# Weight-part rounding spread over eight sequences with its subtraction on GpSimd, biases and first values earlier, and the last-but-one rows through another PSUM bank, in a one-core attention and mixture-of-experts block

## The reference

```python
q = einsum('bse,hed->bhsd', x, Wq) + bq      # k and v likewise, 16 heads of 64
scores = where(causal, q @ k.T / sqrt(64), -inf)
out = softmax(scores) @ v ; out = out.reshape(32, 256, 1024) @ Wo + bo
x = layernorm(x + out)
xn = layernorm_affine(x, gamma, beta)
probs = softmax(xn @ router_w.T / 1.5)       # 8 experts, top 2
y = sum over the two experts of w_e * (silu(xn @ W1[e]) @ W2[e])
x = layernorm(x + y)
```

## Time and profile before

| | us |
|---|---|
| median of 3 runs | 1322.31 (1321.48 to 1324.12) |
| the profiled execution | 1320.37 |
| its span, first to last instruction | 1318.2 |
| PE busy | 1288.0 (98%) |
| DVE busy | 1102.1 (84%) |
| ACT busy | 1078.2 (82%) |
| POOL busy | 498.7 (38%) |

### The profile page before, as it was taken

How to read it: one execution, slowest core, us unless ns; L and a number is a source line. 1 busy time by engine, 2 the same in 40 slices (tenths; PEclk the granted TensorE clock), 3 DMA queues, 4 the chain that set the end, 5 groups by cost and what they waited for, 6 DMA issues and landing times.

```text
span 1318.2 us, 36163 instructions
## 1 busy us (share of the span) xinstructions
PE 1288.0 (98%) x11298; PEld 1141.5 (87%) x11298; DVE 1102.1 (84%) x5209; ACT 1078.2 (82%) x3481; POOL 498.7 (38%) x1067
## 2 busy tenths in 40 slices
PE   7999999999999999999999999999998999999997
PEld 6888888888888888888888888888887999999983
DVE  6888888888888888888888888888886898888856
ACT  7888888888888888888888888888885777777737
POOL 1013333333333333333333333333333675665645
PEclk9999999999999999999999999999998999999999
DMA  5011000000000000000000000000033587777748
GB/s 211 35 67 46 14 14 17 15 18 16 16 14 14 14 14 13 14 14 14 14 14 14 14 18 16 19 16 14 14 140 92 158 239 233 236 226 233 222 137 329
DMA packets 58860, 98.19 MB, mean 74 GB/s; under 512 B 9376, under 2 KB 36131, under 8 KB 58416
## 3 DMA queue, kind: packets, MB, share of 16 engines
q1 hardware_dynamic: 49024, 78.67, 19.2%
q0 software_dynamic: 8640, 17.13, 3.8%
q10 hardware_dynamic: 1008, 0.08, 0.1%
HBM read 65.85 MB, written 30.91 MB: 73 GB/s over the span
## 4 chain that ended last, share of the span: by engine, by line
PE 86%; ACT 6%; DVE 4%; issue 1%; DMA 1%; POOL 0%; ACTq 0%; SPq 0%; POOLq 0%; DVEq 0%
PE ps_f L1102 15%; PE ps_b L1136 13%; PE ps_a L1102 13%; PE ps_s L1143 12%; PE ps_s L1124 9%; PE ps_s L1102 7%; PE ps_a L1327 4%; PE ps_b L1327 4%; PE ps_s L1127 4%; ACT probs L596 2%; PE ps_s L1398 2%; ACT probs L598 2%; PE ps_a L1299 1%; PE ps_s L1148 1%; PE ps_f L1168 1%
## 5 line engine op out<-in xcount | busy, mean ns | idle before, releaser
L596 ACT ACTIVATE probs<-probs,neg_max 128x256 f32<-128x256 f32 x512 | 255.3, 499 | 134.7 <-DVE neg_max L845 134.7
L472 POOL TENSOR_SCALAR ln_b<-mv 128x2 f32<-128x2 f32 x32 | 6.1, 190 | 633.7 <-DVE mv L908 633.7
L841 DVE CUSTOM_DVE_ANT_0 probs<-ps_s,mask 128x256 f32<-128x256 f32 x512 | 214.2, 418 | 29.4 <-PE ps_s L1127 26.9
L1143 PE MATMUL ps_s<-ident,probs 128*128 128x128 f32 x1536 | 200.6, 274 | 0.9 <-issue 0.8
L1136 PE MATMUL ps_b<-pt,f_y 128*64 128x256 f32 (+1 forms) x2048 | 196.9, 334 | 3.5 <-ACT f_y L591 1.6
L598 ACT ACTIVATE probs<-probs,neg_max 128x128 f32<-128x128 f32 x512 | 198.7, 388 | 0.0
L855 DVE TENSOR_SCALAR probs<-probs,inv_sums 128x256 f32<-128x256 f32 x512 | 181.9, 355 | 9.1
L1136 PEld LDWEIGHTS ps_b<-pt,f_y 128*64 128x64 f32 x2048 | 132.6, 137 | 54.4 <-issue 9.6
L562 POOL DMA_INDIRECT y_tok<-f_y,m_dest x142 | 145.8, 1027 | 83.7 <-DVE m_dest L1008 57.2
L1124 PE MATMUL ps_s<-qk 64*128 64x256 f32 x1024 | 170.7, 409 | 5.3 <-ACT pt L631 3.0
L1143 PEld LDWEIGHTS ps_s<-ident,probs 128*128 128x128 f32 x1536 | 173.0, 143 | 1.6 <-issue 1.5
(11 more groups left out here) (205 smaller groups left out, 3144.4 us busy)
## 6 DMA issues: line engine op xcount, KB each, us to landing
m_w<-w_split SPq DMA_DIRECT2D x71, 512.0 KB
m_x<-queue SPq DMA_DIRECT2D x71, 133.0 KB
f_y<-y_tok SPq DMA_DIRECT2D x32, 256.0 KB, 6.6
queue<-empty SPq DMA_DIRECT2D x8, 532.0 KB, 4.8
x_raw<-in_x SPq DMA_DIRECT2D x32, 128.0 KB, 2.1
w_split<-f_y SPq DMA_DIRECT2D x8, 512.0 KB, 3.2
out_x<-f_y SPq DMA_DIRECT2D x16, 256.0 KB, 6.4
y_tok<-f_y,m_dest POOLq DMA_INDIRECT x142
```

Of the source, the lines that this page charges most:

```text
L596: act.activation(row[:, 0:2 * P], row[:, 0:2 * P], ACT.Exp, scale=-1.0, bias=neg_max[:, pair, h, 0:1], accum_out=sums[:, d % 2, pair, h, 0:1])
L841: dve.tensor_tensor_reduce(out=row[:, 0:2 * P], in0=ps_s[:, pair, h, 0:2 * P], in1=mask[:].rearrange("p a b -> p (a b)"), scale=-1.0, scal ...
L1143: ins = pe.transpose(ps_s[:, pair, h, dst:dst + P], probs[:, buf, pair, h, src:src + P], ident[:])
```

## The change

Five pieces.

1. Weight parts: ScalarE rounds one expert per sequence, at the end of step q = 1 of sequences 1 to 8, where eight consecutive steps held one each. The subtraction moves from VectorE to GpSimd's `step`, ahead of `norm`. SP stores the parts at q = 3 of these sequences.
2. Biases: `bq` and `bk` get semaphores of their own. VectorE scales bq first of all; ScalarE's first copy of q and k waits for bk and the scaled bq, and the other five small transfers are waited for later.
3. First values: at d = 0 VectorE copies the first half of the values out of `ps_f` ahead of `normalise(0, 0)`, where it stood behind.
4. The rows of sequence 30 (the last but one, at d = 127) are transposed behind both pairs' probabilities, into `ps_f`, where they stood ahead of them, in `ps_s`. `transpose_x(0)` moves up behind them, ahead of `step_outputs(LAST)`. ScalarE's `xnt` goes behind `first_pt(127)`.
5. On ScalarE `copy_outputs(127)` moves ahead of the second pair's exponentials, and `affine(0)` ahead of `copy_outputs(LAST)` and `first_pt(LAST)`; on VectorE `rest_of_x(0)` moves ahead of `second_pt(LAST)`.

```diff
 # SP
-                if n in (1, 2):
-                    e = d - QUADS
+                if q == 3 and 1 <= n <= E:
+                    e = n - 1
                     sp.wait_ge(w1_lo_done, e + 1)
 # GpSimd
+            def rest_of_w1(e):
+                pool.wait_ge(w1_hi_done, e + 1)
+                if e >= 2:
+                    pool.wait_ge(w1_stored[e % 2], e // 2 * 16)
+                pool.tensor_tensor(w1_part[:, e % 2, 1].bitcast(F32R), w1_raw[:, e], w1_part[:, e % 2, 0], ALU.subtract
+                                  ).then_inc(w1_lo_done, 1)
...
+                if q == 1 and 1 <= n <= E:
+                    rest_of_w1(n - 1)
-            pool.wait_ge(small_loaded, 16 * 7)
+            pool.wait_ge(small_loaded, 16 * 5)
 # ScalarE
+            act.dma_start(bq_raw[:], bq).then_inc(bq_loaded, 16)
+            act.dma_start(bk_sb[:], bk).then_inc(bk_loaded, 16)
...
-            act.wait_ge(small_loaded, 16 * 7)
+            act.wait_ge(bk_loaded, 16)
             act.wait_ge(biases_ready, 1)
             evacuate_qk(0, 0)
             evacuate_qk(0, 1)
+            act.wait_ge(small_loaded, 16 * 5)
...
+                if d == LAST - 1:
+                    copy_outputs(d)
                 if d < LAST:
                     for h in range(2):
                         exponentials(d, 1, h)
-                if q == 3 and n in MID:
+                if d == LAST - 1:
+                    first_pt(d)
+                    act.wait_ge(zt_ready, n)
+                    act.activation(xnt[:], ps_f[:, 0:S], ACT.Identity, scale=gamma_sb[:, 0:1],
+                                   bias=beta_sb[:, 0:1]).then_inc(xnt_done, 1)
+                if q == 3 and 1 <= n < SEQS - 1:
...
-                if n in (1, 2):
-                    e = d - QUADS
+                if q == 1 and 1 <= n <= E:
+                    e = n - 1
                     act.wait_ge(w1_loaded, 16)
...
+            affine(0)
             copy_outputs(LAST)
             first_pt(LAST)
-            affine(0)
             copy_outputs(LAST + 1)
 # VectorE
+            dve.wait_ge(bq_loaded, 16)
+            dve.tensor_scalar(bq_sb[:], bq_raw[:], SCALE, None, ALU.mult).then_inc(biases_ready, 1)
             rest_of_xt(1, 0)
             rest_of_weights(0, 0)
             rest_of_weights(0, 1)
-            dve.wait_ge(small_loaded, 16 * 7)
-            dve.tensor_scalar(bq_sb[:], bq_raw[:], SCALE, None, ALU.mult).then_inc(biases_ready, 1)
             rest_of_weights(0, 2)
+            dve.wait_ge(small_loaded, 16 * 5)
...
+                    if d == 0:
+                        evacuate_first_v(1, 0)
                     normalise(d, 0)
...
-                if n in (1, 2):
-                    rest_of_w1(d - QUADS)
...
+            rest_of_x(0)
             second_pt(LAST)
-            rest_of_x(0)
 # TensorE
-                if q == 3 and n in MID:
+                if q == 3 and 1 <= n < SEQS - 1:
                     pe.wait_ge(z_done, n)
...
+                if d == LAST - 1:
+                    pe.wait_ge(z_done, n)
+                    pe.wait_ge(res_done, n * TILES)
+                    for i in range(TILES):
+                        ins = pe.transpose(ps_f[:, i * P:(i + 1) * P], z[:, (n - 1) % 2, i, 0:D], ident[:])
+                    ins.then_inc(zt_ready, 1)
+                    transpose_x(0)
                 second_filler(n, q)
...
             step_outputs(LAST)
-            transpose_x(0)
             pe.wait_ge(max_done, LAST * 4)
```

More of the change, by code:

```diff
@@ L199, in postln_block @@
         attn_w_loaded = [sem("attn_w_loaded_%d" % i) for i in range(6)]
+        bq_loaded = sem("bq_loaded")
+        bk_loaded = sem("bk_loaded")
         small_loaded = sem("small_loaded")
@@ L577, in _ @@
         def _(act):
-            for dst, src in ((bq_raw, bq), (bk_sb, bk), (bv_sb, bv), (bo_sb, bo), (gamma_sb, gamma),
-                             (beta_sb, beta), (rw_sb, router_wt)):
+            act.dma_start(bq_raw[:], bq).then_inc(bq_loaded, 16)
+            act.dma_start(bk_sb[:], bk).then_inc(bk_loaded, 16)
+            for dst, src in ((bv_sb, bv), (bo_sb, bo), (gamma_sb, gamma), (beta_sb, beta), (rw_sb, router_wt)):
                 act.dma_start(dst[:], src).then_inc(small_loaded, 16)
@@ L656, in step @@
                     evacuate_qk(d + 1, 0)
-                if 1 <= d <= LAST:
+                if 1 <= d < LAST - 1:
                     first_pt(d)
@@ L660, in step @@
                     evacuate_qk(d + 1, 1)
-                if d >= 2 and q == 3:
+                if 2 <= d < LAST - 1 and q == 3:
                     copy_outputs(d)
-                if n in (1, 2):
-                    e = d - QUADS
+                if q == 1 and 1 <= n <= E:
+                    e = n - 1
                     act.wait_ge(w1_loaded, 16)
@@ L738, in rest_of_weights @@
                 ins.then_inc(attn_w_lo, 1)
[L740 to L745, removed]
             def rest_of_xt(count, par):
@@ L970, in step @@
                     rest_of_xt(n + 2, (n + 1) % 2)
-                if q == 0 and n < SEQS:
+                if q == 0 and 1 <= n < SEQS:
                     evacuate_first_v(n * 4 + 1, 0)
@@ L1169, in transpose_input, with transpose_x @@
                 ins.then_inc(xt_ready, 1)
+            def transpose_x(j):
+                pe.wait_ge(m_x_loaded[j % WBUFS], (j // WBUFS + 1) * 16)
+                if j >= 1:
+                    pe.wait_ge(m_xnt_done, j)
+                for i in range(BLOCKS):
+                    ins = pe.transpose(ps_a[:, 0, i * P:(i + 1) * P], m_x[:, j % WBUFS, i, 0:D], ident[:])
+                ins.then_inc(m_xt_ready, 1)
             def first_filler(n, q):
@@ L1292, in _ @@
             sequences(step)
-            def transpose_x(j):
-                pe.wait_ge(m_x_loaded[j % WBUFS], (j // WBUFS + 1) * 16)
-                if j >= 1:
-                    pe.wait_ge(m_xnt_done, j)
-                for i in range(BLOCKS):
-                    ins = pe.transpose(ps_a[:, 0, i * P:(i + 1) * P], m_x[:, j % WBUFS, i, 0:D], ident[:])
-                ins.then_inc(m_xt_ready, 1)
             def hidden(j, chunks=range(CH)):
```

## The result

The changed kernel takes 1308.77 us (median of six runs, 1307.25 to 1311.52), the kernel before beside it 1321.89 (six runs, 1318.85 to 1324.41): a ratio of 0.990 with an interval of 0.9885 to 0.9923. That is 13.1 us less, with an interval of 10.2 to 15.2. The profiled executions stand at 1307.78 against 1320.37 us, spans 1306.0 against 1318.2.

A forecast was written before the change was run, and what follows sets the result against it. TensorE alone was taken to set the pace in steady attention, with gains only where it idles. Weights 4.9, beginning 1.0 and seam 4.4 sum to 10.3 us, so 1322.31 becomes 1312.0 us; range 1309.6 to 1315.5.

The forecast's parts named there:

- Weights: 4.9 said: Weight parts in attention: spreading them and moving the subtraction to GpSimd gives back 4.9 us of TensorE's time.
- upper bound: Weight parts: at most 5.3 us gained, since sequence 1 has no router products and should be shorter.
- the estimate's 0.3 to 0.5 us: Weight parts: sequence 1 estimated 0.3 to 0.5 us shorter than a steady one, for lack of router products.
- four times gave 1.9: Weight parts: GpSimd's subtraction taken as 1.9 us, from four times the elements of a 0.46 us addition.
- 0.20 us for a meeting: Weight parts: a VectorE operation beside GpSimd's work loses 0.20 us; no meeting was expected, so cost nothing.
- Rival D: Weight parts: GpSimd's subtraction holds VectorE, deciding if it lasts some 4.5 us; 1328 us at 5 us each; chance 0.03.
- Beginning: 1.0 said: Beginning: earlier copies of q and of the first values give 1.0 us, bounds 0.5 and 1.1.
- 0.5 us shorter: Beginning: ScalarE's first copy of q starts at 8.9, 0.5 us sooner, and with it scores and exponentials.
- Seam: 4.4 said: Seam between attention and experts: shorter waits and one clock fall left give 4.4 us, bounds 2.7 and 5.7.
- rival A: Seam: the clock does not fall, so 5.7 us gained instead of 4.4, time 1310.7 us; chance 0.30.
- likelier than not: Seam: the clock still falls once, adding 0.94 us for the outputs and some 0.4 for transposes.
- Rival C: Seam: tokens landing after 1009.96 cost a us per us late; 1316.4 us with the gain gone; chance 0.05.

The follow-up runs named there:

- early products: The changed kernel with 28 unread bf16 products of 128x128 at TensorE's start, where it was idle: 1307.45 us, ratio 0.9892.
- filled waits: The changed kernel with early products and seven unread products around transpose_x(0) at the new seam: 1395.56 us on a slower chip, ratio 0.9929.
- (filled): The kernel before with unread products put into five waits of TensorE, at the beginning and the seam: 1317.72 us, ratio 0.9972.
- undone tokens' part: The changed kernel with transpose_x(0), affine(0) and rest_of_x(0) back in their old places: 1311.79 us, ratio 0.9925.
- threefold subtraction: The changed kernel with GpSimd's subtraction of the weight parts done three times over in each of eight sequences: 1309.76 us, ratio 0.9904.

## Why the prediction was off by 3 us

**Weights: 4.9 said, 5.3 to 5.4 measured, in the changed kernel and alone.** The mechanism was right, both that ScalarE's share hides at the turn to q = 2 and that GpSimd's work has room. The size came out at the upper bound, as it would if sequence 1 is shorter than a steady one by the estimate's 0.3 to 0.5 us and more: twelve steps took 0.7 us less than three steady sequences. The subtraction took 1.27 us, where four times gave 1.9. The conflict was priced at 0.20 us for a meeting and is what is left of GpSimd's instruction; it cost nothing because they do not meet, and next to nothing at three times the length. Rival D's mechanism is real, its threshold of 4.5 us was not tried.

**Beginning: 1.0 said, 0.1 in the profiled pair, 1.3 in the mean over six traces with the old beginning and six with the new one (without early products).** Two steps failed. The prediction took the time until the first scores, and with it ScalarE's chain, as 0.5 us shorter; in the changed kernel's trace the projections' half pace until 10.2 us took that back (9.55 against 9.41), and TensorE's 1.94 us came back as 1.87 ahead of step 1's scores. And it priced the clock at nothing here, which one trace could not correct. Step 4's scores started at 40.42 to 40.67 us in five of six executions with the old beginning, and at 39.21 in the one that the prediction was made from; with the new one at 38.45 to 39.10 in five without the early products, and at 40.20 in the sixth. From the first scores to those of step 4 it took 29.89 to 30.02 where the clock fell and 28.91 and 28.92 where it did not; with the new order 28.32 to 28.78 in seven executions, and 29.60 in the one where it fell. So from the first scores on the new order gives 0.1 to 0.6 us by itself, and the rest is 1.0 us of clock that usually comes with it, and the bias, which gives by how late the seventh transfer is. No run takes the copy of the first values and the bias apart. The chain of the prediction was somewhat too generous, and the clock was the larger term.

**Seam: 4.4 said, 5.9 measured, the value of rival A.** The sentence that failed is that a fall of the clock is "likelier than not". With the new order it fell in two of eight traces (and not in a ninth, with filled waits), with the old one once or twice in all three. With the clock up the old seam takes 15.85 us (filled) and the new one 13.3 to 13.45: 2.5 us are waits. The rest, 1.7 to 3.3, is clock. The profiled execution of before had the longest seam of its kind; in the mean over these three and eight traces the seam takes 18.4 and 13.8 us, a gain of 4.5. That this is near the forecast's 4.4 is luck: the forecast set one fall against two. The undone tokens' part shows 1.65 of the 2.5 by itself. Rival C, tokens that land late, did occur as scatter (waits of 0.86 to 2.46 us); in the changed kernel the wait for `pt` covered it, while with the threefold subtraction and the filled seam the outputs of 126 came 0.65 and 1.3 us later for it.

**The sum.** The profiled pair differs by 12.2 us of span, of which 11.4 are the three terms (5.4, 0.1 and 5.9). In the mean over the traces they are 5.4, 1.3 and 4.5, together 11.2. The medians of the times differ by 13.1, with an interval of 10.2 to 15.2, which holds all of these and, just, the forecast's 10.3. So up to 1.9 us of the 13.1 belong to no term that I can name, and may be noise. The range failed at its low end by its last step: it added the three largest gains, 12.1 us, but only 0.5 us for the scatter of the medians, where the ratio's interval reaches some 2.5 us to either side.

## What to carry to other kernels

A wait of TensorE of 1 to 2.5 us costs its length and, in some executions, microseconds at half clock behind it; a single trace shows one throw of that chance, so look at two or three before a stage is priced, and count the usual fall in what the wait's removal gives. See, too, whether a wait that is taken away comes back ahead of the next instruction, as 1.94 us did here as 1.87. Work that must be done early goes where the chain that feeds TensorE has idle time, on each engine that it uses: spreading it or moving it alone gave half or less. When GpSimd takes over elementwise work, place it so that it ends before VectorE's plain scaling begins; beside the masks it cost nothing.

## What the hardware showed that I had not expected

- TensorE starts at half pace, until 7.5 to 10.2 us by execution, while the views print a granted clock of 1.00: the traces have no entry of it until the rise. With 28 small products from 1.45 us on the first entry stands at 4.6 and 5.6 us.
- On one chip both kernels took some 84 us more at a mean granted clock of 0.991. In attention, where 36 us of them were lost, nearly all of the loss stands at one place: once a sequence, at q = 0, ScalarE and VectorE both pause. The waits, summed over the changed kernel on that chip (us in total, times, the longest):

```profile
DVE f_y L876 <- remote: 49.5, 27, 1.9
...
ACT f_y L639 <- remote: 36.9, 25, 4.5
```

27 pauses of VectorE with 49.5 us, which cost TensorE about 1.2 us each (8.07 us a step against 7.76). The trace names no releaser in the program ("remote"). All four traces from that chip have such rows, and none of the ten from other chips. What it is stays open; the ratio is the same, 0.9911 there and 0.990 here.
- From the second half of `hidden(0)` to the end, which no edit touched, the ten executions on other chips took between 295.1 and 298.7 us, by waits for gathered tokens and for the last sums' loads. Edits under that size cannot be read from a span, only from their own stretch.
